# Selective scan: three PSUM banks for the decay factors, one for the row of C, written between the two sums of an index

## The chip, the cores and the metric

The kernel runs on one core of a Trainium2 chip. The metric is device time in microseconds, the median of several executions. The profile is one execution, recorded by the hardware profiler; its times start at the first instruction of the span.

## The reference

The program is a two-layer hybrid model over 16 sequences (batches b) of 512 tokens with 128 channels: attention, a recurrent feed-forward, a selective state space block, the recurrent feed-forward again, then latent attention, experts, rotary attention, experts. Only the state space block matters here, and in it only the scan:

```
def step(h, inp):
    dt_t, B_t, C_t, x_t = inp
    dA = jnp.exp(dt_t[..., None] * A[None])
    dBx = dt_t[..., None] * B_t[:, None, :] * x_t[..., None]
    h = dA * h + dBx
    y_t = jnp.sum(h * C_t[:, None, :], axis=-1)
    return (h, y_t)
...
y = jnp.moveaxis(ys, 0, 1) + Dp * xc
y = y * _silu(z)
return jnp.einsum('bti,di->btd', y, out_proj_w)
```

There are 256 inner channels and 16 state indices n. B and C have 16 rows each for a batch, one for each index, shared by all channels; A is a number for each channel and index.

## The kernel before, in words

`mamba_scan` takes the batches one after another. The 512 tokens of a batch lie along the free dimension and the 256 channels lie on 128 partitions in two halves h = 0 and 1. For each index n and half h, numbered k = 2 (16 b + n) + h, this is done:

- TensorE copies a row of B to all 128 partitions: a matmul of a selection matrix in bf16 with the three-part bf16 rows, into the one bank `b_ps` (`broadcast_b`, L1932). ScalarE copies it to SBUF (`copy_b`, L1994) into a ring of eight.
- ScalarE computes the decay factor exp(A dt) of the half into a bank of `da` in PSUM (L2032). `da` has RA = 2 banks.
- GpSimd multiplies the row of B with dt x (L2097) into `dbx`, a ring of eight.
- VectorE runs the recurrence over the tokens (`scan`, L2139) and multiplies the state with the row of C (`times_c`, L2148), which it reads straight from PSUM. TensorE has put that row there (`broadcast_c`, L1938); `c_ps` has two banks, index n uses bank n % 2.
- TensorE adds the product to the half's sum in `y_ps` with an identity matmul in fp32, which the trace shows as two passes (L1963).

Every engine runs an order written out by hand, with semaphores between the engines. The orders that matter:

- TensorE, for each n: `broadcast_b` of n + 4 (AHEAD), `broadcast_c` of n + 1, the sum of half 0, the sum of half 1; after n = 9 and n = 11 (SKIP_AT) a matmul that adds D x to one half (L1967); after n = 4 the output projection of the batch before (`outward`, L1945). `b_ps` has one bank, so a row of B waits for the copy of the one before.
- ScalarE, for each n: `copy_b` of n + 3 (COPIED), then the decay factors of (n, 0) and (n, 1). A decay factor waits until the scan that read its bank is done: `scanned` at R - RA + k + 1, where R = 8 is added at the start. From n = 4 to 10 the softplus of the next batch is strewn between.
- VectorE, for each n: the scans of both halves, then both products. At n = 0 two gates of the batch before stand between scans and products (L2155), after n = 6 the residual add (L2159), after n = 13 two step sizes of the next batch (L2130).
- GpSimd, for each n: the two products `dbx`, and the products of the next batch's set-up after n = 11 and n = 14.

`prod_ready` counts finished products (with RS = 4 added at the start), `acc_mm` finished sums, `c_mm` rows of C. The eight banks of PSUM are all taken: `da` 2, `b_ps` 1, `c_ps` 2, `y_ps` 2, `out_ps` 1. Batches 2 to 13 run in a loop of two batches a turn, the first two and the last two are written out.

Of the kernel before, what the change touches and what calls it, by code (L numbers as in the profile page):

```python
# [1843 lines left out]
def mamba_scan(core, x, mamba_dram, bc_dram, w):  # L1844
# [3 lines left out]

    R = 8
    RS = 4  # L1850
    RA = 2
    RB = 8
    AHEAD = 4
    COPIED = 3
# [2 lines left out]
    with core.phase() as ph:  # L1857
# [10 lines left out]
        state, prod = ph.sb("state", [P, RS, T]), ph.sb("prod", [P, RS, T])  # L1868
        gated = ph.sb("gated", [P, 2, T])
        da = ph.ps("da", [P, RA, T])  # L1870
        b_ps, c_ps = ph.ps("b_ps", [P, T]), ph.ps("c_ps", [P, 2, T])
        y_ps, out_ps = ph.ps("y_ps", [P, 2, T]), ph.ps("out_ps", [P, T])
        loaded = [ph.sem(f"loaded{u}") for u in range(2)]
        select_loaded = ph.sem("select_loaded")
# [20 lines left out]
        def k_slot(n, h, ring=R):  # L1895
            return (2 * n + h) % ring
# [22 lines left out]
        @block.tensor  # L1919
        def _(pe):  # L1920
            pe.sem_inc(acc_mm, RS)
            pe.sem_inc(out_mm, 1)

            def inputs_loaded(b, u):
                pe.wait_ge(loaded[u], 32 * (b // 2) + 32 if isinstance(b, int) else 16 * (b - u) + 32)

            def broadcast_b(b, u, n):

                if n == 0:
                    inputs_loaded(b, u)  # L1930
                pe.wait_ge(b_ready, STATE * b + n + 1)
                pe.matmul(b_ps[:, :], w["select"][:, n], bc[:, u], start=True, stop=True).then_inc(b_mm, 1)  # L1932

            def broadcast_c(b, u, n):
                if n == 0:
                    inputs_loaded(b, u)
                pe.wait_ge(prod_ready, RS - 4 + 2 * (STATE * b + n) + 2)
                pe.matmul(c_ps[:, n % 2], w["select"][:, STATE + n], bc[:, u], start=True, stop=True  # L1938
                          ).then_inc(c_mm, 1)

            def outward(b):
                pe.wait_ge(gated_ready, 2 + 2 * b + 2)
                pe.wait_ge(added, b + 1)
                for h in range(2):
                    mm = pe.matmul(out_ps[:, :], w["out_w"][:, h], gated[:, h], start=(h == 0), stop=(h == 1))  # L1945
                mm.then_inc(out_mm, 1)

            def sequence(b, u, first=False, last=False):
                for n in range(STATE):
                    if n + AHEAD < STATE:  # L1950
                        broadcast_b(b, u, n + AHEAD)
                    elif not last:
                        broadcast_b(b + 1, 1 - u, n + AHEAD - STATE)
                    if n + 1 < STATE:
                        broadcast_c(b, u, n + 1)
                    elif not last:
                        broadcast_c(b + 1, 1 - u, 0)
                    for h in range(2):
                        k = 2 * (STATE * b + n) + h
                        if n == 0 and not first:  # L1960
                            pe.wait_ge(gated_ready, 2 * b + h + 1)
                        pe.wait_ge(prod_ready, RS + k + 1)
                        pe.matmul(y_ps[:, h], w["ident"], prod[:, k_slot(n, h, RS)], start=(n == 0),  # L1963
                                  stop=(n == STATE - 1)).then_inc(acc_mm, 1)
                    if n in SKIP_AT:
                        h = SKIP_AT.index(n)
                        pe.matmul(y_ps[:, h], skip_w[:, h], inp[:, u, h], start=False, stop=False)  # L1967
                    if n == 4 and not first:
                        outward(b - 1)

            pe.wait_ge(select_loaded, 16)
            for n in range(AHEAD):
                broadcast_b(0, 0, n)
            broadcast_c(0, 0, 0)
            pe.wait_ge(skip_ready, 2)
            sequence(0, 0, first=True)
            sequence(1, 1)
            with pe.Fori(1, NB // 2 - 1) as i:
                for u in range(2):
                    sequence(2 * i + u, u)  # L1980
            sequence(NB - 2, 0)
            sequence(NB - 1, 1, last=True)
            outward(NB - 1)

        @block.scalar
        def _(act):
            act.preload_act_table_set("natural_log_exp_and_others")
            act.sem_inc(b_ready, 1)

            def copy_b(b, n):  # L1990
                m = STATE * b + n
                act.wait_ge(b_mm, m + 1)
                act.wait_ge(dbx_ready, 2 * m + 2)
                act.activation(b_sb[:, n % RB], b_ps[:, :], ACT.Copy).then_inc(b_ready, 1)  # L1994

            act.activation(rate[:, :, :], w["a_log"], ACT.Exp).then_inc(soft, 1)

            def magnitude(b, u, h):
                act.wait_ge(loaded[u], 32 * (b // 2) + 32 if isinstance(b, int) else 16 * (b - u) + 32)
                act.wait_ge(dt_ready, 2 * b + h + 1)  # L2000
                act.activation(small[:, h], inp[:, u, 4 + h], ACT.Abs).then_inc(soft, 1)

            def decayed(b, h):
                act.wait_ge(soft, 1 + 6 * b + 3 * h + 1)
                act.activation(small[:, h], small[:, h], ACT.Exp, scale=-1.0).then_inc(soft, 1)

            def rounded(b, h):
                act.wait_ge(soft, 1 + 6 * b + 3 * h + 2)
                act.activation(lost[:, h], small[:, h], ACT.Identity, bias=w["one"]).then_inc(back, 1)

            def returned(b, h):
                act.wait_ge(back, 4 * b + 2 * h + 1)
                act.activation(lost[:, h], lost[:, h], ACT.Identity, bias=w["one"], scale=-1.0
                               ).then_inc(back, 1)

            def logarithm(b, h):
                act.wait_ge(soft, 1 + 6 * b + 3 * h + 2)
                act.activation(log1[:, h], small[:, h], ACT.Ln, bias=w["one"]).then_inc(soft, 1)

            def sequence(b, u, last=False):  # L2020
                for n in range(STATE):
                    m = STATE * b + n
                    if n + COPIED < STATE:
                        copy_b(b, n + COPIED)
                    elif not last:
                        copy_b(b + 1, n + COPIED - STATE)
                    for h in range(2):
                        k = 2 * m + h
                        if n == 0:
                            act.wait_ge(dt_ready, 2 + 2 * b + h + 1)  # L2030
                        act.wait_ge(scanned, R - RA + k + 1)
                        act.activation(da[:, k_slot(n, h, RA)], dt[:, u, h], ACT.Exp, scale=rate[:, h, n:n + 1]  # L2032
                                       ).then_inc(da_ready, 1)
                    if last:
                        continue
                    if n == AT:
                        magnitude(b + 1, 1 - u, 0)
                    if n == AT + 1:
                        decayed(b + 1, 0)
                        rounded(b + 1, 0)  # L2040
                    if n == AT + 2:
                        returned(b + 1, 0)
                    if n == AT + 3:
                        logarithm(b + 1, 0)
                        magnitude(b + 1, 1 - u, 1)
                    if n == AT + 4:
                        decayed(b + 1, 1)
                    if n == AT + 5:
                        rounded(b + 1, 1)
                        returned(b + 1, 1)  # L2050
                    if n == AT + 6:
                        logarithm(b + 1, 1)

            act.wait_ge(rate_ready, 1)
            for h in range(2):
                magnitude(0, 0, h)
                decayed(0, h)
                rounded(0, h)
                returned(0, h)
                logarithm(0, h)  # L2060
            for n in range(COPIED):
                copy_b(0, n)
            with act.Fori(0, NB // 2 - 1) as i:
                for u in range(2):
                    sequence(2 * i + u, u)
            sequence(NB - 2, 0)
            sequence(NB - 1, 1, last=True)

# [46 lines left out]
        def _(dve):  # L2115
# [26 lines left out]
            def times_c(b, n, h):  # L2142
                k = 2 * (STATE * b + n) + h
                s = k_slot(n, h, RS)
                dve.wait_ge(scanned, R + k + 1)
                dve.wait_ge(c_mm, STATE * b + n + 1)
                dve.wait_ge(acc_mm, k + 1)
                dve.tensor_tensor(prod[:, s], state[:, s], c_ps[:, n % 2], ALU.mult).then_inc(prod_ready, 1)  # L2148

            def gate(b, u):  # L2150

# [247 lines left out]
```

## Time and profile before

| | us |
|---|---|
| median of 3 runs | 5323.51 |
| lowest and highest | 5317.22 and 5327.42 |
| profiled execution, device time | 5320.46 |
| its span, first to last instruction | 5318.7 |
| mean granted TensorE clock of the span | 0.914 of 2.4 GHz |

In the page of the profile, busy shares are of the whole span of eleven phases; the scan is one of them, about a fifth of the span. A share of the page says little about it, so the views are cut to its stretch. In these views PE is TensorE's matmuls, PEld its weight loads, DVE VectorE, ACT ScalarE, POOL GpSimd. L12 is line 12 of the kernel. The time between brackets behind a row is how long the engine had stood idle before it, and what ended that.

### The profile page before, as it was taken

The numbers are of one execution on the slowest core, as the hardware profiler recorded it, in microseconds if no ns is written. First come the engines' busy times: TensorE is split into PE (matmuls) and PEld (weight loads), VectorE is DVE, ScalarE is ACT, GpSimd is POOL, SyncE is SP. The second block draws the span as 40 slices with busy tenths as digits, with TensorE's granted clock in tenths as the row PEclk, the third lists the DMA queues.
The fourth block names the chain that finished last, engine by engine and source line by source line (L and its number), as shares of the span: only waits on it lengthen the run. The fifth ranks groups of instructions, "written<-read, shape, count | busy, mean of one in ns | idle before, by whom it ended". The sixth has DMA issues, their size and how long they took to land. (4 is left out here: it accounts for less than half of the span.)

```text
span 5318.7 us, 109649 instructions
## 1 busy us (share of the span) xinstructions
PE 4172.8 (78%) x31637; PEld 2106.4 (40%) x31638; DVE 3541.8 (67%) x8801; ACT 2850.0 (54%) x5331; POOL 1612.8 (30%) x1559
## 2 busy tenths in 40 slices
PE   6499999898667677778789999933987699983598
PEld 3144444552222222226222222323983244442497
DVE  3388888647899998984499999831116788873012
ACT  7255555676555555556667777721325466662232
POOL 3000000011777777741200000055536000006552
PEclk9699999999899998999889999966999799995799
DMA  7522222106100010000722222213665333321466
GB/s 257 150 73 72 74 76 72 33 0 216 42 26 26 26 36 28 26 13 2 244 73 74 78 76 75 72 38 123 214 189 209 108 95 96 98 77 46 142 212 191
DMA packets 546193, 502.03 MB, mean 94 GB/s; under 512 B 163774, under 2 KB 482911, under 8 KB 545788
## 3 DMA queue, kind: packets, MB, share of 16 engines
q1 hardware_dynamic: 527724, 460.95, 29.2%
q0 software_dynamic: 18160, 37.42, 2.1%
q8 instruction: 137, 2.24, 0.2%
q14 instruction: 172, 1.41, 0.1%
HBM read 330.57 MB, written 167.58 MB: 94 GB/s over the span
## 5 line engine op out<-in xcount | busy, mean ns | idle before, releaser
L1428 ACT ACTIVATE p_probs<-p_t_ps 128x512 f32<-128x512 f32 (+1 forms) x2304 | 1141.8, 551 | 680.9 <-PE p_t_ps L1320 243.8
L1963 PE MATMUL p_y_ps<-p_prod,c_ident 128*128 128x512 f32 x1024 | 554.5, 667 | 295.5 <-DVE p_prod L2148 290.9
L1333 PE MATMUL p_o_ps<-p_probs,p_v_st 128*32 128x256 f32 (+3 forms) x8704 | 727.0, 407 | 3.2 <-ACT p_o_sb L1414 2.9
L1465 DVE TENSOR_REDUCE p_row_max<-p_s_ps 128x1 f32<-128x512 f32 x1072 | 669.0, 680 | 71.9 <-PE p_s_ps L1271 55.6
L1254 POOL TENSOR_TENSOR p_v_st<-p_v_raw,p_ones 128x128 f32<-128x128 f32 x192 | 87.5, 456 | 2068.4 <-PE p_o_ps L1333 1946.9
L2097 POOL TENSOR_TENSOR p_dbx<-p_dtx,p_b_sb 128x512 f32<-128x512 f32 x512 | 632.4, 1267 | 113.2 <-ACT p_b_sb L1994 112.4
L2139 DVE TENSOR_TENSOR_SCAN p_state<-p_da,p_dbx 128x512 f32<-128x512 f32 x512 | 598.8, 1208 | 84.6 <-ACT p_da L2032 67.0
L1302 PE MATMUL p_t_ps<-p_t_q,p_t_k 50*128 50x512 bf16 (+3 forms) x3072 | 516.4, 336 | 147.6 <-ACT p_probs L1428 58.6
L1271 PE MATMUL p_s_ps<-p_s_k,p_s_q 48*128 48x512 bf16 (+3 forms) x3216 | 508.6, 340 | 146.8 <-DMA p_s_k<-stack_k 75.0
L1462 DVE CUSTOM_DVE_ANT_0 p_tried<-p_s_ps,p_s_bias 128x512 bf16<-128x512 f32 (+3 forms) x1072 | 470.5, 485 | 137.0 <-PE p_s_ps L1271 134.4
L1462 DVE CUSTOM_DVE_ANT_0 p_tried<-p_s_ps,c_mask_row 128x512 bf16<-128x512 f32 (+3 forms) x1072 | 470.5, 485 | 86.2 <-PE p_s_ps L1271 76.2
L791 DVE TENSOR_TENSOR p_y<-p_out_ps,p_raw 128x256 f32<-128x256 f32 x142 | 60.3, 425 | 581.3 <-PE p_out_ps L742 581.3
L1963 PEld LDWEIGHTS p_y_ps<-p_prod,c_ident 128*128 128x128 f32 x1024 | 188.7, 202 | 556.9 <-DVE p_prod L2148 478.3
L1994 ACT ACTIVATE p_b_sb<-p_b_ps 128x512 f32<-128x512 f32 x256 | 152.6, 596 | 430.2 <-PE p_b_ps L1932 419.4
L1302 PEld LDWEIGHTS p_t_ps<-p_t_q,p_t_k 50*128 50x128 bf16 x3072 | 149.1, 93 | 563.6 <-ACT p_probs L1428 361.5
L803 POOL DMA_INDIRECT weighed_rows<-p_y,p_raw x284 | 273.1, 962 | 296.9 <-DVE p_y L791 252.4
L2032 ACT ACTIVATE p_da<-p_dt,p_rate 128x512 f32<-128x512 f32 x512 | 337.4, 686 | 29.5 <-DVE p_state L2139 28.6
L773 ACT ACTIVATE p_hidden<-p_hid_ps 128x512 f32<-128x512 f32 x284 | 169.6, 597 | 316.0 <-PE p_hid_ps L731 313.7
L2148 DVE TENSOR_TENSOR p_prod<-p_state,p_c_ps 128x512 f32<-128x512 f32 x512 | 322.3, 670 | 0.0
L1312 PE MATMUL p_t_ps<-p_bias_parts,c_flip 64*128 64x384 bf16 (+2 forms) x4608 | 302.8, 269 | 0.0
L654 POOL DMA_INDIRECT routed_rows<-p_rows,p_index x256 | 249.2, 974 | 163.3 <-DVEq L599 86.5
L1333 PEld LDWEIGHTS p_o_ps<-p_probs,p_v_st 128*32 128x32 f32 x8704 | 174.7, 108 | 262.0 <-issue 245.4
(256 smaller groups left out, 6888.0 us busy)
## 6 DMA issues: line engine op xcount, KB each, us to landing
p_wb<-in_w SPq DMA_DIRECT2D x142, 512.0 KB
p_s_q<-stack_q SPq DMA_DIRECT2D x408, 96.0 KB
p_s_k<-stack_k SPq DMA_DIRECT2D x408, 96.0 KB
p_t_q<-stack_q SPq DMA_DIRECT2D x390, 96.0 KB
p_t_k<-stack_k SPq DMA_DIRECT2D x390, 96.0 KB
mamba_inputs<-p_out SPq DMA_DIRECT2D x17, 1536.0 KB, 5.7
p_inp<-mamba_inputs SPq DMA_DIRECT2D x17, 1536.0 KB
stack_q<-p_parts SPq DMA_DIRECT2D x51, 384.0 KB
```

Source lines behind the costliest of these rows:

```text
L1271: mm = pe.matmul(s_ps[:, banks[r], at:at + width], s_q[rows, g % 2, pair, c * P:(c + 1) * P], s_k[rows, g % 2, pair, 0:width], start=True, ...
L1302: mm = pe.matmul(out[r], t_k[rows, g % 2, pair, c * P:(c + 1) * P], t_q[rows, g % 2, pair, first:first + width], start=True, stop=not mask ...
L1312: mm = pe.matmul(out[r], bias["flip"][rows, k], bias["t"][q][rows, k, 2 * g + pair, first - c * P:first - c * P + width], start=False, sto ...
L1333: mm = pe.matmul(o_ps[32 * j:32 * j + 32, at:to], v_st[:, g % 2, c, j, :], probs[:, g % 2, j, place[c] + at - first:place[c] + to - first] ...
L1428: act.activation(exps, tile, ACT.Exp, scale=scale).then_inc(expd, 1)
L1462: read = dve.tensor_tensor_reduce(tried[:, slot, at:at + width], scores, over, 1.0, LOWEST, ALU.add, ALU.max, found)
L1465: read = dve.tensor_reduce(found, scores, X, ALU.max)
L1963: pe.matmul(y_ps[:, h], w["ident"], prod[:, k_slot(n, h, RS)], start=(n == 0), stop=(n == STATE - 1)).then_inc(acc_mm, 1)
L2032: act.activation(da[:, k_slot(n, h, RA)], dt[:, u, h], ACT.Exp, scale=rate[:, h, n:n + 1]).then_inc(da_ready, 1)
L2097: pool.tensor_tensor(dbx[:, k_slot(n, h)], dtx[:, u, h], b_sb[:, n % RB], ALU.mult).then_inc(dbx_ready, 1)
L2139: dve.tensor_tensor_scan(out=state[:, out], data0=da[:, k_slot(n, h, RA)], data1=dbx[:, s], initial=0.0, op0=ALU.mult, op1=ALU.add).then_i ...
L2148: dve.tensor_tensor(prod[:, s], state[:, s], c_ps[:, n % 2], ALU.mult).then_inc(prod_ready, 1)
```

## The change

`da` gets three banks and `c_ps` one. The row of C for n + 1 is no longer written ahead of both sums of n; its matmul stands between the sum of half 0 and the sum of half 1, behind a wait for both products of n. The decay factor waits for the scan three halves back, at n = 0 two back, since the ring of three starts anew with each batch.

```
-    RA = 2
+    RA = 3
...
-        b_ps, c_ps = ph.ps("b_ps", [P, T]), ph.ps("c_ps", [P, 2, T])
+        b_ps, c_ps = ph.ps("b_ps", [P, T]), ph.ps("c_ps", [P, T])
...
             def broadcast_c(b, u, n):
                 if n == 0:
                     inputs_loaded(b, u)
-                pe.wait_ge(prod_ready, RS - 4 + 2 * (STATE * b + n) + 2)
-                pe.matmul(c_ps[:, n % 2], w["select"][:, STATE + n], bc[:, u], start=True, stop=True
+                pe.wait_ge(prod_ready, RS + 2 * (STATE * b + n))
+                pe.matmul(c_ps[:, :], w["select"][:, STATE + n], bc[:, u], start=True, stop=True
                           ).then_inc(c_mm, 1)
...
                         broadcast_b(b + 1, 1 - u, n + AHEAD - STATE)
-                    if n + 1 < STATE:
-                        broadcast_c(b, u, n + 1)
-                    elif not last:
-                        broadcast_c(b + 1, 1 - u, 0)
                     for h in range(2):
                         k = 2 * (STATE * b + n) + h
                         if n == 0 and not first:
                             pe.wait_ge(gated_ready, 2 * b + h + 1)
                         pe.wait_ge(prod_ready, RS + k + 1)
+                        if h == 1 and n + 1 < STATE:
+                            broadcast_c(b, u, n + 1)
+                        elif h == 1 and not last:
+                            broadcast_c(b + 1, 1 - u, 0)
                         pe.matmul(y_ps[:, h], w["ident"], prod[:, k_slot(n, h, RS)], start=(n == 0),
                                   stop=(n == STATE - 1)).then_inc(acc_mm, 1)
...
-                        act.wait_ge(scanned, R - RA + k + 1)
+                        act.wait_ge(scanned, R - (RA if n else 2) + k + 1)
...
-                dve.tensor_tensor(prod[:, s], state[:, s], c_ps[:, n % 2], ALU.mult).then_inc(prod_ready, 1)
+                dve.tensor_tensor(prod[:, s], state[:, s], c_ps[:, :], ALU.mult).then_inc(prod_ready, 1)
```

## Rows read from the trace of the kernel before

**Rows 1.** Engines over stretches: stretch, length, busy us (instructions), clock, DMA.

```profile
1734.30:1737.90 3.60, 3.57 (x4) 1.33 (x5) 3.60 (x5) 0.00 (x0) 3.60 (x3) 0.50 0.69 215
...
1339.00:2369.00 1030.00, 727.08 (x1664) 266.61 (x1664) 936.12 (x1104) 560.25 (x925) 756.69 (x608) 0.93 0.08 26
```

**Rows 2.** Grouped instructions of the scan: busy, mean ns, idle before and releasers.

```profile
L2139 DVE TENSOR_TENSOR_SCAN p_state<-p_da,p_dbx 128x512 f32<-128x512 f32 x512 | 598.8, 1208 | 84.6 <-ACT p_da L2032 67.0 <-issue 9.0 <-POOL p_dbx L2097 8.5
...
L2148 DVE TENSOR_TENSOR p_prod<-p_state,p_c_ps 128x512 f32<-128x512 f32 x512 | 322.3, 670 | 0.0
...
L1963 PEld LDWEIGHTS p_y_ps<-p_prod,c_ident 128*128 128x128 f32 x1024 | 188.7, 202 | 556.9 <-DVE p_prod L2148 478.3 <-issue 65.7 <-DVE p_gated L2155 9.9
...
L1938 PEld LDWEIGHTS p_c_ps<-p_bc,xn 96*128 96x128 bf16 x254 | 26.7, 105 | 96.2 <-issue 85.0 <-DVE p_prod L2148 11.2
```

**Rows 3.** Who waited for whom in the scan: us in total, times, longest.

```profile
ACT p_b_sb L1994 <- PE p_b_ps L1932: 417.2, 228, 5.4
...
DVE p_state L2139 <- ACT p_da L2032: 67.0, 70, 1.7
...
ACT p_da L2032 <- DVE p_state L2139: 28.6, 54, 3.1
```

**Rows 4.** An ordinary step in order of time: start, length, engine, line.

```profile
1745.71 1.26 DVE L2148 TENSOR_TENSOR p_prod<-p_state,p_c_ps 128x512 f32<-128x512 f32 x2
...
1746.42 1.98 PE L1963 MATMUL p_y_ps<-p_prod,c_ident 128*128 128x512 f32 x4 [1.01 <-DVE p_prod L2148]
...
1748.24 0.38 PE L1932 MATMUL p_b_ps<-p_bc,xn 96*128 96x512 bf16 x1
...
1748.46 0.38 PE L1938 MATMUL p_c_ps<-p_bc,xn 96*128 96x512 bf16 x1
...
1748.74 0.60 ACT L1994 ACTIVATE p_b_sb<-p_b_ps 128x512 f32<-128x512 f32 x1 [1.09 <-PE p_b_ps L1932]
...
1749.24 1.30 ACT L2032 ACTIVATE p_da<-p_dt,p_rate 128x512 f32<-128x512 f32 x2
...
1749.85 1.98 PE L1963 MATMUL p_y_ps<-p_prod,c_ident 128*128 128x512 f32 x4 [1.01 <-DVE p_prod L2148]
...
1750.31 2.33 DVE L2139 TENSOR_TENSOR_SCAN p_state<-p_da,p_dbx 128x512 f32<-128x512 f32 x2
```

**Rows 5.** The step with the output projection, in order of time.

```profile
1751.67 1.88 PE L1945 MATMUL p_out_ps<-p_gated,c_out_w 128*128 128x512 f32 x4
...
1753.39 0.38 PE L1932 MATMUL p_b_ps<-p_bc,xn 96*128 96x512 bf16 x1
...
1754.38 1.29 ACT L2032 ACTIVATE p_da<-p_dt,p_rate 128x512 f32<-128x512 f32 x2
...
1755.25 2.34 DVE L2139 TENSOR_TENSOR_SCAN p_state<-p_da,p_dbx 128x512 f32<-128x512 f32 x2 [1.44 <-ACT p_da L2032]
```

**Rows 6.** A step with a skip product, in order of time.

```profile
1705.95 1.02 PE L1967 MATMUL p_y_ps<-p_inp,p_skip_w 128*128 128x512 f32 x2
...
1708.68 2.34 DVE L2139 TENSOR_TENSOR_SCAN p_state<-p_da,p_dbx 128x512 f32<-128x512 f32 x2 [0.58 <-ACT p_da L2032]
```

**Rows 7.** Behind a batch boundary, in order of time.

```profile
1734.33 3.78 PE L1963 MATMUL p_y_ps<-p_prod,c_ident 128*128 128x512 f32 x4 [4.31 <-DVE p_prod L2148]
...
1737.90 0.63 PE L1932 MATMUL p_b_ps<-p_bc,xn 96*128 96x512 bf16 x1
...
1738.33 0.63 PE L1938 MATMUL p_c_ps<-p_bc,xn 96*128 96x512 bf16 x1
...
1738.66 0.60 ACT L1994 ACTIVATE p_b_sb<-p_b_ps 128x512 f32<-128x512 f32 x1 [5.43 <-PE p_b_ps L1932]
...
1740.03 2.34 DVE L2139 TENSOR_TENSOR_SCAN p_state<-p_da,p_dbx 128x512 f32<-128x512 f32 x2 [1.73 <-ACT p_da L2032]
```

**Rows 8.** The skip step of another batch: decay pair and scan.

```profile
1907.79 1.29 ACT L2032 ACTIVATE p_da<-p_dt,p_rate 128x512 f32<-128x512 f32 x2
...
1909.02 2.34 DVE L2139 TENSOR_TENSOR_SCAN p_state<-p_da,p_dbx 128x512 f32<-128x512 f32 x2 [0.93 <-ACT p_da L2032]
```

## The prediction

> **What bounds the kernel now.** I read the views from the outside in. The table of engines over stretches of the span comes first. The diff touches the scan phase alone, so I cut to it, 1339 to 2369 us, where VectorE is busy 936 of 1030 us and TensorE 727 [rows 1]. VectorE is the engine to follow. The grouped list of VectorE's instructions says how much it stands still: 84.6 us before its scans and nothing at all before its products with C [rows 2]. The list of waits says for whom: 67.0 us in 70 waits for ScalarE's decay factor (L2032) [rows 3]. ScalarE in turn waited 417.2 us for the row of B out of TensorE (L1932), but only 28.6 us for a scan to free a bank of `da` [rows 3]. So before costing anything: the ring of `da`, which the change lengthens, is the short wait, and the row of B, whose place in TensorE's queue the change alters, is the long one.
>
> The timeline shows how the two hang together. An ordinary step of an index n takes 3.43 us (sums begin at 1746.42 and again at 1749.85) [rows 4]. In it TensorE starts the two sums 0.71 us after the products begin (1746.42), starts the row of B 1.82 us later (1748.24), ScalarE copies that row 0.50 us after (1748.74), and starts the decay pair 0.50 us after that (1749.24) [rows 4]. ScalarE is in order, so `copy_b(n+3)` stands ahead of the exponential that the scan of n needs. How soon may the scan follow? Where it did wait, it began 0.87 us after the decay pair began (1754.38 to 1755.25) [rows 5]. From products to the scan two indices on, that chain is 0.71 + 1.82 + 0.50 + 0.50 + 0.87 = 4.40 us; VectorE's own work between the same two points is 1745.71 to 1750.31, 4.60 us [rows 4]. The ordinary step therefore hides the chain with 0.20 us to spare, and no more.
>
> It doesn't hide where TensorE has something extra before the row of B. With the output projection (n = 4) B starts at 1753.39, after 1.72 us more, and the scan stalls 1.44 us [rows 5]; there are 15 such, of 1.20 to 1.44 us. With a skip product (n = 9 and 11) B starts two passes of 0.43 us later and the scan stalls 0.58 us [rows 6]; 31 such, of 0.34 to 0.93 us. Just after a batch boundary TensorE has stood idle 4.31 us, its granted clock in the next 3.6 us is 0.50, that is 1.2 GHz, B follows the start of the sums after 3.57 us instead of 1.82, and the scan stalls 1.73 us [rows 1, 7]; 14 stalls of this kind at index 2 and about 10 at other places. These are the 70 waits.
>
> **The change part by part.** *Moving C's row.* TensorE's order was B(n+4), C(n+1), sum 0, sum 1; it becomes B(n+4), sum 0, C(n+1), sum 1. No instruction is added or taken away: 256 rows of C, 256 of B, 1024 passes of the sums as before. But C used to run while TensorE was going to wait for a product anyway: after C at 1748.46 its next work came at 1749.85 [rows 4]. Now it runs between the sums, in front of sum 1 and all that is queued behind it: skip product, output projection, and B(n+5). Its price is the distance from B to C at full clock, 1748.24 to 1748.46, 0.22 us [rows 4]; at half clock 1737.90 to 1738.33, 0.43 us [rows 7]. Is there a gap between the sums that it could fill? The projection, which is four passes as the two sums are, takes 1.72 us to the start of B, four times 0.43 [rows 5], and the sums take the same after a start of 0.10; so there is none. Its own weight load should hide: C may go once the second product is done, which is 1.26 us after the products begin, while sum 0 ends at about 0.71 + 0.10 + 0.86 = 1.67 us [rows 4].
>
> What each place pays, by kind of stall: 15 projections at 0.22 = 3.3 us. Skips: of 31, six have a stall of 0.93 us whose scan starts 1.23 us after its decay pair (1907.79 to 1909.02) where 0.87 would do [rows 8], so something of VectorE's own, 0.36 us long, covers the delay there; the other 25 at 0.22 = 5.5 us. The 24 stalls at half clock: between 0.22 and 0.43 each, since the clock often rises within the same pair; I take 0.33 = 8 us, ends 5.3 and 10.3. One gate that waits for sum 1 of the batch before: 0.4 us. An ordinary step loses its 0.20 us of slack to a 0.22 us delay; a stall of 0.02 us then gives the next step cover, so at most one in two of some 80 steps without other cover pays: under 1 us. Sum 3.3 + 5.5 + 8 + 0.4 + 0.8 = 18 us. What remains just hidden is worth naming: VectorE's extra instructions (gates, step sizes, the residual add) cover indices 0, 1, 7, 8, 14 and 15.
>
> *One bank for C.* C(n+1) can no longer be written before both products of n are read. It must be there when VectorE wants it, 3.43 us after the products of n began. At full clock it is: it starts at about 1.67 us and a consumer follows 0.50 us after a start (B at 1748.24, copy at 1748.74) [rows 4], so 2.2 us, with 1.2 us to spare. At half clock sum 0 takes 1.71 + 0.15 us, C starts at 0.71 + 1.86 = 2.57 us and its reader may follow 0.76 us later (1737.90 to 1738.66) [rows 7]: 3.33 us, 0.1 us to spare. Cost nothing; if this cover goes, it is the rival below. Perfetto Trace Analysis of the Trainium skill, section Matmuls, speaks against this edit: independent matmul groups should rotate through different PSUM banks, so that one is read out while the next is written. By that rule the reader of each of 256 rows of C would wait out the 0.50 us from its start to its use, 128 us in all; by the arithmetic on the rows above it waits for none. No run here shows it yet.
>
> *Three banks for the decay factors.* The exponential of (n, 0) now waits for the scan three halves back, not two. That removes up to 28.6 us of ScalarE's waiting [rows 3]. None of it, as far as I can see, is on the path. In the ordinary step the decay pair starts 1.00 us after the row of B and runs on; in the step of the projection, whose scan stalls, 0.99 us after it [rows 4, 5]: had a scan held it there, it would have come later. The copy is held by TensorE, and a third bank doesn't bring the row of B any sooner. Ends: 0 and 28.6 us saved; I take 0, by these two rows. At n = 0 the code keeps a distance of two.
>
> The profiled execution took 5320.5 us, 1.8 beyond its span and 3.1 below the median of 5323.5. 5320.5 + 18 = 5338.5 on its own footing, 5341 against the median.
>
> **Rivals.**
> (a) *The third bank pays.* If ScalarE, freed from waiting for scans, kept a lead over VectorE, the stalls would shrink. For it: 54 such waits, 28.6 us. Against: ScalarE's lead ends at each copy, which waited 228 times for TensorE [rows 3]. Its price is at most 28.6 us, so 5323.5 - 28.6 = 5295 us if C's delay also hid; it outweighs the delay once more than 18 of the 28.6 us lie on the path. This one ends faster.
> (b) *The delay vanishes.* If C's row in fact finds a hole between the sums, because the second product comes late, the time stays at 5323.5. For it: the second product is done only 0.4 us before sum 0 ends, by the 1.26 and 1.67 us above. Against: that is still before.
> (c) *C's weight load isn't hidden*, or the single bank makes C miss its reader. Each step would pay C's load and the reload for sum 1 on top, 0.105 + 0.202 us, about 0.3 [rows 2]. 64 stalled steps x 0.3 = 19 us, and the ordinary steps, their slack gone, some three per batch x 16 x 0.3 = 14 us: 5341 + 33 = 5374 us. Against: the load may start at 1.26 us and is wanted at 1.67.
>
> **How the numbers follow.** Forecast, the row of B comes later by C's time: 0.68, centre 5341. (a) 0.08, (b) 0.14, (c) 0.10; of the last, 0.02 is for a wait of 0.50 us on every row of C, 256 x 0.50 = 128 us on top. Within the forecast the half-clock stretches, which account for about 27 us of stalls before, may fall otherwise: 8 us either way, which with the bounds gives 5327 to 5352. The range 5321 to 5364 takes in the forecast, (b) and the lower part of (c). A measurement of this kernel can tell about 0.2%, 10.6 us, from no change. Faster by that: (a), 0.08. Slower: 0.93 of the forecast and (c), 0.63 + 0.10 = 0.73. Same: 0.19.
>
> **What would show it.** In the profile after, on TensorE the order sum 0, C, sum 1, with B's row 2.04 us after the sums begin instead of 1.82 in an ordinary step. VectorE's stall after the projection grows from 1.44 to about 1.66 us, after a skip from 0.58 to 0.80 us; its idle time before scans goes from 84.6 to about 102 us, and the idle time before the products with C stays near nothing. ScalarE's wait for a scan falls from 28.6 us to less than half while VectorE's time doesn't follow. The forecast is wrong if the stalls keep their sizes, if the products begin to wait for C (rival c), or if scans that waited for the decay factor no longer do (rival a).

## The result and the profile after

| | before, us | after, us |
|---|---|---|
| median | 5322.15 (5 runs) | 5374.41 (5 runs) |
| lowest and highest | 5317.08 and 5327.42 | 5369.56 and 5378.81 |
| span of the profiled execution | 5318.7 | 5372.6 |
| mean granted TensorE clock of the span | 0.914 | 0.906 |

The ratio is 1.0100, with an interval of 1.0086 to 1.0114: 52 us slower. The forecast was slower, 5341 us, in a range of 5321 to 5364. The sign is right; the loss was put at a third of what it is, and the measured time lies outside the range.

The groups of VectorE's instructions in the scan after the change (columns as in [rows 2]), then the waits (as in [rows 3]), then the stretch of 1030 us (as in [rows 1]):

```profile
L2139 DVE TENSOR_TENSOR_SCAN p_state<-p_da,p_dbx 128x512 f32<-128x512 f32 x512 | 598.9, 1208 | 132.7 <-ACT p_da L2032 118.5 <-POOL p_dbx L2097 9.7 <-issue 4.4
L2148 DVE TENSOR_TENSOR p_prod<-p_state,p_c_ps 128x512 f32<-128x512 f32 x512 | 322.1, 669 | 0.0
```

```profile
DVE p_state L2139 <- ACT p_da L2032: 118.5, 83, 2.8
...
ACT p_da L2032 <- DVE p_state L2139: 7.9, 8, 2.5
```

```profile
1339.00:2369.00 1030.00, 725.10 (x1582) 266.52 (x1583) 894.21 (x1053) 534.16 (x893) 735.97 (x592) 0.89 0.08 26
```

VectorE's idle time before scans went from 84.6 to 132.7 us [rows 2], by 48.1 of the 53.9 us that the span grew. The scan phase, from the start of its first scan to the end of its last product, grew by 49.2 us, from 1012.9 to 1062.1; the other 4.7 us lie outside it, in work that the change doesn't touch, and are no more than runs of one kernel differ by. VectorE's work itself is the same to 0.2 us. Nothing waits for C: the products' idle time is 0.0, with one bank as with two. ScalarE's waits for a scan fell from 28.6 us in 54 to 7.9 us in 8 [rows 3], so the third bank did its part, and VectorE's time didn't follow. The clock's mean over the stretch fell from 0.93 to 0.89 [rows 1].

An ordinary step after the change, on TensorE:

```profile
1782.99 1.12 PE L1963 MATMUL p_y_ps<-p_prod,c_ident 128*128 128x512 f32 x2 [2.12 <-DVE p_prod L2148]
...
1783.96 0.38 PE L1938 MATMUL p_c_ps<-p_bc,xn 96*128 96x512 bf16 x1
...
1784.18 1.02 PE L1963 MATMUL p_y_ps<-p_prod,c_ident 128*128 128x512 f32 x2
...
1785.04 0.38 PE L1932 MATMUL p_b_ps<-p_bc,xn 96*128 96x512 bf16 x1
```

Sum 0, C, sum 1, B. C starts 0.97 us after the first sum, as the two passes end, and the second sum 0.22 us later; B comes 2.05 us after the sums begin, where it was 1.82 [rows 4]. The stalls that answer to [rows 5] and [rows 6]:

```profile
1771.46 2.34 DVE L2139 TENSOR_TENSOR_SCAN p_state<-p_da,p_dbx 128x512 f32<-128x512 f32 x2 [1.66 <-ACT p_da L2032]
...
1791.18 2.34 DVE L2139 TENSOR_TENSOR_SCAN p_state<-p_da,p_dbx 128x512 f32<-128x512 f32 x2 [0.77 <-ACT p_da L2032]
```

1.44 became 1.66 and 0.58 became 0.77 us: the delay of C's 0.22 us arrives at VectorE, as forecast. It isn't the whole story. I added up VectorE's stalls before scans from the timeline by the index at which they stand, over all 16 batches:

| index n | before, us | after, us | difference |
|---|---|---|---|
| 0 (batch boundary, turns of the loop) | 16.9 | 25.0 | 8.1 |
| 2 | 17.9 | 24.0 | 6.1 |
| 6 (projection) | 20.9 | 24.3 | 3.4 |
| 8 and 9 | 7.0 | 12.5 | 5.5 |
| 11 (skip) | 8.5 | 11.7 | 3.2 |
| 13 (skip) | 10.3 | 32.2 | 21.9 |
| 15 | 3.0 | 3.1 | 0.1 |

Index 6 and 11 carry what the forecast gave them. Index 8, which the forecast counted among the places that VectorE's extra instructions cover, stalls in 13 batches. Index 13 carries 21.9 us, which the forecast didn't foresee: in 11 of the 16 batches its stall is 2.49 to 2.85 us. This is one, in order of time:

```profile
1725.65 1.12 PE L1963 MATMUL p_y_ps<-p_prod,c_ident 128*128 128x512 f32 x2 [1.86 <-DVE p_prod L2148]
...
1726.62 0.56 PE L1938 MATMUL p_c_ps<-p_bc,xn 96*128 96x512 bf16 x1
...
1726.97 1.91 PE L1963 MATMUL p_y_ps<-p_prod,c_ident 128*128 128x512 f32 x2
...
1728.68 1.73 PE L1967 MATMUL p_y_ps<-p_inp,p_skip_w 128*128 128x512 f32 x2
...
1730.24 0.38 PE L1932 MATMUL p_b_ps<-p_bc,xn 96*128 96x512 bf16 x1
...
1732.11 2.34 DVE L2139 TENSOR_TENSOR_SCAN p_state<-p_da,p_dbx 128x512 f32<-128x512 f32 x2 [2.50 <-ACT p_da L2032]
```

```profile
1725.80:1730.20 4.40, 4.40 (x7) 1.66 (x8) 3.82 (x5) 0.00 (x0) 2.36 (x2) 0.61 0.00 0
```

The second sum takes 1.71 us to the start of the skip product, twice its 0.86, the skip product 1.56: B comes 4.59 us after the first sum, and the scan stalls 2.50 us. The granted clock over those 4.40 us is 0.61, so most of them pass at the lower level, 1.2 GHz. Added up from the record of the granted clock, the scan spent 126 us at half clock before and 201 us after. Both leave out its first 7 to 8 us, which are at half clock in every run.

### The profile page after: what moved, and what is told of

Same layout as the page of the kernel before. It is cut to its first block and busy times, and to the rows that moved or that the text cites. A ratio compares the mean times of both kernels' runs of the same rounds, so it can differ in the third digit from the quotient of the medians.

```text
span 5372.6 us, 109718 instructions
## 1 busy us (share of the span) xinstructions
PE 4217.9 (79%) x31637; PEld 2123.6 (40%) x31638; DVE 3542.0 (66%) x8801; ACT 2843.3 (53%) x5331; POOL 1616.0 (30%) x1559
## 5 line engine op out<-in xcount | busy, mean ns | idle before, releaser
L1963 PE MATMUL p_y_ps<-p_prod,c_ident 128*128 128x512 f32 x1024 | 621.6, 692 | 311.9 <-DVE p_prod L2148 310.5
L2139 DVE TENSOR_TENSOR_SCAN p_state<-p_da,p_dbx 128x512 f32<-128x512 f32 x512 | 598.9, 1208 | 132.7 <-ACT p_da L2032 118.5
L1271 PE MATMUL p_s_ps<-p_s_k,p_s_q 48*128 48x512 bf16 (+3 forms) x3216 | 509.1, 340 | 145.0 <-DMA p_s_k<-stack_k 74.1
```

The lines of the kernel that those rows point to most:

```text
L1271: mm = pe.matmul(s_ps[:, banks[r], at:at + width], s_q[rows, g % 2, pair, c * P:(c + 1) * P], s_k[rows, g % 2, pair, 0:width], start=True, ...
L2139: dve.tensor_tensor_scan(out=state[:, out], data0=da[:, k_slot(n, h, RA)], data1=dbx[:, s], initial=0.0, op0=ALU.mult, op1=ALU.add).then_i ...
```

## The experiments

Three parts of the change could carry the loss: the order of TensorE (theory O), the ring of decay factors (R), the single bank of C (S). Within O, the loss beyond the 18 us of the forecast could be the clock's (K). And if so, the clock could react to the slower pace (P) or to C's place among the sums (Q). The runs were made in four sets, each with its own runs of the kernel before beside it, whose medians were 5273.2, 5273.7, 5320.7 and 5321.3 us. So ratios are compared, not times. The sets differ outside the scan phase: the rest of the profiled execution takes 4258 to 4266 us in the first two sets and 4306 to 4315 us in the other two and the first measurement. So the length of the scan phase alone can be compared across sets. "Half clock" is the time of the scan at half clock, added up as above; "idle" is VectorE's before scans; "phase" is the length of the scan phase. The last three come from one profiled execution of each run. "Order alone" below is the changed kernel with `RA = 2`.

| run | ratio | interval | idle, us | half clock, us | phase, us |
|---|---|---|---|---|---|
| before, first measurement | 1 | | 84.6 | 126 | 1012.9 |
| the change, first measurement | 1.0100 | 1.0086 to 1.0114 | 132.7 | 201 | 1062.1 |
| e8, the change again | 1.0089 | 1.0072 to 1.0106 | 135.8 | 205 | 1065.9 |
| e1, order alone | 1.0094 | 1.0077 to 1.0111 | 133.1 | 198 | 1063.0 |
| e6, place alone, two banks of C | 1.0099 | 1.0082 to 1.0116 | 133.1 | 201 | 1062.7 |
| e2, before, copy behind | 0.9867 | 0.985 to 0.9883 | 16.9 | 72 | 938.7 |
| e3, after, copy behind | 0.9866 | 0.985 to 0.9883 | 17.0 | 68 | 939.1 |
| e4, before, filled | 0.9979 | 0.9969 to 0.9988 | 74.1 | 61 | 1001.4 |
| e5, order alone, filled | 1.0016 | 1.0007 to 1.0026 | 91.3 | 92 | 1018.9 |
| e7, two rows of C between | 1.0105 | 1.0088 to 1.0122 | 135.0 | 167 | 1067.0 |
| e9, small copy on ScalarE | 1.0046 | 1.0029 to 1.0063 | 109.5 | 184 | 1038.3 |
| e10, two small copies | 1.009 | 1.0073 to 1.0107 | 129.1 | 205 | 1059.1 |
| e11, copy behind and filled | 0.9862 | 0.9846 to 0.9879 | 16.9 | 58 | 938.7 |

**Which part: the ring?** The ring of decay factors put back to two:

```
-    RA = 3
+    RA = 2
```

> The change with the ring of decay factors put back to two banks: C in one bank, written between the two sums, is all that is left. Theory O (the order of TensorE, with what its clock makes of it): the ring of three does nothing, so 5374 us within 5, VectorE idle before scans about 130 us, as with the whole change. Theory R (the third bank of decay factors does harm, for instance by moving ScalarE's work): a good part of the loss goes, 5322 to 5350 us. If the third bank helped and hid part of the loss: above 5385 us.

> The changed kernel as it stands, once more, on the chip that ran the order alone. If the third bank of decay factors does nothing, its ratio to before is that of the order alone, 1.009, within 0.002. If the third bank gives something back or takes it: 0.3% or more away.

The order alone costs 1.0094, the whole change 1.0089 and 1.0100. The two ran on different chips, not on one as the second expectation has it, so each is compared with the kernel before beside it; their scan phases, 1063.0 us for the order alone and 1062.1 and 1065.9 us for the change, say the same. ScalarE's waits for a scan are back at 36.9 us in 88 in the order alone, against 7.9 us; VectorE's idle time is the same within 3 us. The third bank removes waits that nobody is waiting behind. R falls.

**Which part: the single bank?** The kernel before with nothing but the place of C changed; two banks of C stay:

```
-                    if n + 1 < STATE:
-                        broadcast_c(b, u, n + 1)
-                    elif not last:
-                        broadcast_c(b + 1, 1 - u, 0)
...
                         pe.wait_ge(prod_ready, RS + k + 1)
+                        if h == 1 and n + 1 < STATE:
+                            broadcast_c(b, u, n + 1)
+                        elif h == 1 and not last:
+                            broadcast_c(b + 1, 1 - u, 0)
```

> The kernel before with C's matmul between the two sums and nothing else changed: C keeps its two banks, the ring its two. Theory O (place alone): the whole loss, ratio 1.009, idle time before scans about 130 us. Theory S (the single bank takes part): clearly less, 1.003 to 1.006.

```profile
L2139 DVE TENSOR_TENSOR_SCAN p_state<-p_da,p_dbx 128x512 f32<-128x512 f32 x512 | 598.9, 1208 | 133.1 <-ACT p_da L2032 118.9 <-POOL p_dbx L2097 9.8 <-issue 4.4
```

The place alone has the whole loss, 1.0099, and VectorE's idle time is that of the change. The products waited for nothing there either. The single bank costs nothing that these runs can see.

**Is B's row the path?** ScalarE's copy of B's row moved behind the two decay factors, in the kernel before (e2) and in the changed one (e3):

```
-                    if n + COPIED < STATE:
-                        copy_b(b, n + COPIED)
-                    elif not last:
-                        copy_b(b + 1, n + COPIED - STATE)
                     for h in range(2):
...
                                        ).then_inc(da_ready, 1)
+                    if n + COPIED < STATE:
+                        copy_b(b, n + COPIED)
+                    elif not last:
+                        copy_b(b + 1, n + COPIED - STATE)
```

> The kernel before, with one edit: ScalarE's copy of B's row n + 3 stands behind the two decay factors of n, not ahead of them. Theory O says that all of VectorE's 67 us of waits for the decay factor come through this copy, which waits for B's row: they should nearly vanish (under 10 us), half clock or not, and the time falls by about 60 us to 5262 (5250 to 5275). The stalls at the turn of the loop, 17 us at index 0, stay. If the waits have another source (the ring of two, the scan itself), the time stays near 5322 us.

> The changed kernel with the same edit: the copy behind the two decay factors. Theory O: with the copy off the path C's new place costs nothing, so the time is that of the kernel before with the same edit, within 10 us (about 5262). Theory S (the single bank makes C miss its reader where the clock is at half): products wait for C in half-clock stretches and it is 15 to 40 us slower than that one, 5277 to 5300 us, with the idle time in front of VectorE's products, not of its scans.

VectorE's group in e2, then its two groups in e3:

```profile
L2139 DVE TENSOR_TENSOR_SCAN p_state<-p_da,p_dbx 128x512 f32<-128x512 f32 x512 | 599.9, 1213 | 16.9 <-POOL p_dbx L2097 12.5 <-issue 4.4
```

```profile
L2139 DVE TENSOR_TENSOR_SCAN p_state<-p_da,p_dbx 128x512 f32<-128x512 f32 x512 | 599.8, 1213 | 17.0 <-POOL p_dbx L2097 12.6 <-issue 4.4
L2148 DVE TENSOR_TENSOR p_prod<-p_state,p_c_ps 128x512 f32<-128x512 f32 x512 | 324.1, 677 | 0.3 <-PE p_c_ps L1938 0.3
```

The releaser "ACT p_da" is gone from the list, with its 67.0 us. Every wait of VectorE for a decay factor came through the copy in front of it. Both kernels are 70 us faster than before, and they are the same: with the copy off the path, C's place, its single bank and the third bank together cost 0.3 us of waiting (the medians, 5202.96 and 5203.59, can't be told apart). The single bank's price shows here and is that 0.3 us, one wait at a half-clock stretch, so S falls too.

**The clock.** Two more rows of 0.22 us per index where TensorE is idle anyway. In the kernel before (e4) C's row is written three times in its old place; in the order alone (e5) two rows go into the free bank behind B's:

```
+                for _ in range(2):
+                    pe.matmul(c_ps[:, n % 2], w["select"][:, STATE + n], bc[:, u], start=True, stop=True)
                 pe.matmul(c_ps[:, n % 2], w["select"][:, STATE + n], bc[:, u], start=True, stop=True
                           ).then_inc(c_mm, 1)
```

```
                 pe.matmul(b_ps[:, :], w["select"][:, n], bc[:, u], start=True, stop=True).then_inc(b_mm, 1)
+                for _ in range(2):
+                    pe.matmul(fill_ps[:, :], w["select"][:, n], bc[:, u], start=True, stop=True)
```

> The kernel before, with each row of C written three times in a row into the same bank instead of once: 2 x 0.22 us more work for TensorE per index, put where it is idle for 1.0 us, ahead of the sums and behind B's row. Nothing that VectorE waits for moves at full clock. Theory K (a large part of the loss is half-clock stretches that come from TensorE's idle time): the half-clock time of the scan falls from 126 us, the clock's mean in the scan rises from 0.93, and the time falls to 5300 to 5315 us. If the clock doesn't react to it: 5322 us within 5; if the filling gets in the way: above 5330 us.

> The order of the change (one bank of C, written between the sums, two banks of decay factors), and behind each row of B two more rows of 0.22 us into the bank that is free, where TensorE is otherwise idle for about a microsecond. It is the filling of the filled kernel of before, so the two differ by C's place alone. Theory K (the direct cost of C's place is the predicted 18 us, the rest of the loss is more time at half clock): the stalls at index 6 and 11 stay at 1.66 and 0.77 us, the large ones at index 13 and those at 8 shrink towards 0.8 and 0, half-clock time falls from about 200 us to under 100, and the time is 15 to 25 us above the filled kernel of before, a ratio to before of 1.001 to 1.003. If the loss is not the clock's, the kernel stays at a ratio of 1.009.

The stretch of 1030 us in e4, then the stall at index 13 of batch 2 in e5:

```profile
1339.00:2369.00 1030.00, 813.44 (x2204) 314.09 (x2205) 938.37 (x1109) 570.80 (x940) 756.55 (x607) 0.96 0.08 26
```

```profile
1525.10 2.34 DVE L2141 TENSOR_TENSOR_SCAN p_state<-p_da,p_dbx 128x512 f32<-128x512 f32 x2 [1.15 <-ACT p_da L2034]
```

Work that nobody needs makes the kernel before 12.5 us faster by the medians, through the clock: TensorE is busy 813 us of the stretch instead of 727, and the clock's mean is 0.96 instead of 0.93 [rows 1]. In the order alone it takes 0.8% off, 1.0094 to 1.0016; the stalls of 2.5 to 2.85 us at index 13 are gone and those at index 8 too. What is left between the two filled kernels is 5281.3 - 5260.7 = 20.6 us (two sets, whose medians of the kernel before are 0.5 us apart), 17.2 us of idle time and 17.5 us of the scan phase by the profiles. That is C's place with less help of the clock, 31 us more at half clock instead of 75, and it is near the forecast's 18 us. K holds. One more thing stands in the last row: that stall was 0.93 us before, where the forecast let 0.36 us of cover hide the delay. It is 1.15, 0.22 more. The cover didn't hide the delay.

**More of the same delay.** C's row twice between the sums:

```
+                pe.matmul(c_ps[:, :], w["select"][:, STATE + n], bc[:, u], start=True, stop=True)
                 pe.matmul(c_ps[:, :], w["select"][:, STATE + n], bc[:, u], start=True, stop=True
                           ).then_inc(c_mm, 1)
```

> The order of the change with C's row written twice between the sums, so B's row comes another 0.22 us later. Directly: 64 stalled places x 0.22 = 14 us, and now the ordinary steps have no slack left, some three per batch x 16 x 0.22 = 10 us: 24 us over the order alone, a ratio to before of 1.014. If half-clock time grows with the stalls, as theory K has it, another 10 to 30 us: 1.016 to 1.020. If the loss is not in B's delay: 1.009.

```profile
1496.13 2.34 DVE L2140 TENSOR_TENSOR_SCAN p_state<-p_da,p_dbx 128x512 f32<-128x512 f32 x2 [0.16 <-DVE p_prod L2149]
...
1504.94 2.34 DVE L2140 TENSOR_TENSOR_SCAN p_state<-p_da,p_dbx 128x512 f32<-128x512 f32 x2 [1.88 <-ACT p_da L2033]
```

```profile
1339.00:2369.00 1030.00, 755.72 (x1817) 284.31 (x1817) 890.06 (x1046) 540.34 (x892) 732.06 (x588) 0.91 0.08 26
```

The direct part came, if smaller than expected: the stall after the projection is 1.88 us, 0.22 more, and 21 scans of ordinary steps that never waited now wait 0.16 us, 3.3 us in all. The total did not: 1.0105 where 1.014 and more was expected by every theory that puts the loss in B's delay. The interval even takes in the 1.009 that was named for a loss that isn't there; the longer stalls, and e2 and e3, speak against that. Half-clock time fell from 198 to 167 us and gave the direct part back. But this run changes two things at once. The second row of C delays B, and it is also 0.22 us more work for TensorE per index: TensorE is busy 756 us of the stretch, 723 in the order alone. In e4 and e5 such work alone lowered half-clock time. So the fall to 167 us may be the filling's, and e7 doesn't say what more delay by itself does.

**The same delay elsewhere.** The kernel before with TensorE's order untouched, and one small copy of 32 columns on ScalarE (e9), or two (e10), between its wait for B's row and the copy:

```
                 act.wait_ge(dbx_ready, 2 * m + 2)
+                act.activation(junk[:, n % RB], rate[:, :, :], ACT.Copy)
+                act.activation(junk2[:, n % RB], rate[:, :, :], ACT.Copy)
```

> The kernel before, TensorE's order untouched; ScalarE does a small copy of 32 columns between its wait for B's row and the copy of that row, some 0.2 us. The delay is then the same as the change's, but on ScalarE. Theory P (the pace: longer stalls of VectorE leave TensorE idle longer, and its clock goes down more often): stalls grow by about 0.2 us each, half-clock time grows from 126 towards 200 us, large stalls appear at index 8 and 13, ratio 1.007 to 1.010. Theory Q (the place of C among the sums is what the clock reacts to): the direct part alone, 18 to 25 us, half-clock time as before, ratio 1.003 to 1.005.

> The kernel before with two of the small copies on ScalarE between its wait for B's row and the copy. One of them delayed the decay factor by 0.11 us and made the kernel 0.46% slower; two should delay it by 0.22 us or a little more, the change's own delay, with TensorE's order still untouched. Theory P (the pace): the ratio of the change, 1.009 within 0.002, half-clock time about 200 us, the stall after the projection 1.66 to 1.75 us. Theory Q (the place among the sums adds its own): no more than 1.006.

The stall at index 13 of batch 2 in e9, then the stalls after the projection and at index 13 in e10:

```profile
1526.78 2.34 DVE L2141 TENSOR_TENSOR_SCAN p_state<-p_da,p_dbx 128x512 f32<-128x512 f32 x2 [2.74 <-ACT p_da L2034]
```

```profile
1500.84 2.34 DVE L2142 TENSOR_TENSOR_SCAN p_state<-p_da,p_dbx 128x512 f32<-128x512 f32 x2 [1.67 <-ACT p_da L2035]
...
1531.17 2.34 DVE L2142 TENSOR_TENSOR_SCAN p_state<-p_da,p_dbx 128x512 f32<-128x512 f32 x2 [2.86 <-ACT p_da L2035]
```

The single copy delayed the decay factor by 0.11 us (the stall after the projection is 1.55 us), half of what I had meant. By its time e9 falls where Q had put it, 1.0046 and 25 us, and outside P's 1.007 to 1.010. But Q's number is met by chance, since it supposed twice the delay and half-clock time as before: the 25 us that it costs are far more than 70 stalls x 0.11 = 8 us, half-clock time is 184 us, and the large stall at index 13 is there. With the change's own delay, e10 has the change's ratio, its idle time, its half-clock time and its stalls, without a single instruction of TensorE moved. P holds and Q falls: the clock reacts to the delay wherever it stands, not to C's place. With TensorE's own work as it was, half-clock time goes from 126 us without a delay to 184 at 0.11 us and 198 to 205 at 0.22 us. These times are of one profile each, but the mean granted clocks of all runs go the same way: 0.911 to 0.916 in the runs of the kernel before beside them, 0.907 to 0.910 in e9, 0.906 to 0.909 in e10.

**Both edits that helped.**

> The kernel before with both edits that helped: ScalarE's copy behind the decay pair, and two more rows of C in TensorE's idle time. With the copy off the path the clock has nothing left to cost (VectorE's idle time before scans was 17 us, the turns of the loop), so the filling brings nothing more: the ratio of the copy edit alone, 0.987, within 0.002. If half-clock stretches still cost something there: 0.984 or less.

0.9862 against 0.9867: the same, as are the scan phases, 938.7 us both. With the copy behind the pair the clock has nothing left to cost that these runs can see. The version to keep is e2, the kernel before with four lines moved, 1.3% faster than before and 2.3% faster than the changed kernel.

## Why the prediction was right or wrong

- *The bound and the path* (VectorE, held by the decay factor, held by the copy, held by B's row): right. e2 removes the copy from it, and 67.0 us of waits vanish.
- *C's price at full clock, 0.22 us, with its weight load hidden*: right. B comes 2.05 us after the sums where 2.04 was said, the stalls are 1.66 and 0.77 us where 1.66 and 0.80 were said.
- *The ordinary step just keeps hiding the chain*: right for the change; with a second 0.22 us it no longer does (e7).
- *VectorE's extra instructions cover indices 0, 1, 7, 8, 14 and 15*: wrong at 8 and 0. Where TensorE is at half clock the cover is too short: index 8 stalls 0.68 to 1.04 us in 13 batches, and the waits for the decay factor at index 0 grew from 2.4 to 13.6 us.
- *The six skip stalls of 0.93 us have cover*: wrong by 6 x 0.22 = 1.3 us. In the filled pair they went from 0.93 to 1.15. The 0.36 us seem to be added behind the decay factor, not beside it; why, these traces don't show.
- *The 24 stalls at half clock grow by 0.22 to 0.43 us each, 8 us in all, and otherwise "may fall otherwise: 8 us either way"*: this is the step that failed. I took the number of half-clock stretches as given and let it vary evenly around that, as if the delay itself did not act on the clock. It does: half-clock time grew from 126 to 201 us here, and to 205 us where the same delay was put on ScalarE (e10). Of the 48.1 us at the scans, index 6 and 11 and some 3.4 us of index 13 are 10 us of the direct part; the filled pair, whose half-clock time differs by only 31 us, puts the whole of the forecast's mechanism at 17 to 21 us, with the half-clock stalls at 0 and 2 as the rest of it. The other 30 us are new half-clock stretches and their stalls: 18.5 us of them at index 13, the rest at 0, 2 and 8. (The forecast's own lower end, 5327, doesn't follow from its bounds either: 5341 - 8 - 2.7 is 5330; nothing hangs on it.)
- *The third bank pays nothing*: right (e1 against e8 and the first measurement). Rival (a) falls.
- *C reaches its reader from one bank*: right, e6 against e1, and 0.3 us in e3. The rule of the Trainium skill (Perfetto Trace Analysis, section Matmuls) that matmul groups should rotate through different PSUM banks would have given 128 us; no run here agrees. At full clock the row has 1.2 us to spare; at half clock the forecast left it 0.1 us, and there the products do begin to wait, 0.3 us in e3 and, with two rows, 1.1 us in e7, of which the profile puts 0.3 us to C.
- *Rival (b)*, the delay vanishes: falls. *Rival (c)* has the measured time as its number, 5374 us, and is wrong all the same: C's weight load is hidden (C 0.97 us after the first sum, the second sum 0.22 us after that) and no product waits. A number met by chance proves no mechanism.

What stays open: what exactly makes the clock fall. A delay of 0.11 us brings 184 us at half clock, 0.22 brings 198 to 205, 0.44 together with 0.22 us more work of TensorE brings 167, and filling 0.43 us per index without a delay brings 61. That the delay raises half-clock time is shown by e10 and e9; that it does so by leaving TensorE idle for longer is an inference from these runs and not shown, and why the stretches settle at certain indices isn't known. The Trainium skill (TensorE: Matmul & The Clock Gate, section "A second HAM failure mode: psum-queue depth-cycling") tells of a kernel in which short idle times between groups of matmuls made the clock swing between its two levels; the trace agrees as far as that goes, with 201 us at half clock in 52 stretches against 126 us in 28.

## What to carry to other kernels

When a wait on the critical path grows and TensorE idles in that wait, price the stretches at half clock again and let the range reach further upward than downward; they grew by 75 us here and nearly tripled a loss of some 18 us. An experiment that lengthens a delay by more work on TensorE changes the clock by that work too (e7); put the delay on another engine, as e10 does. Follow a stall back through each in-order queue to the first instruction that is needed later than the one behind it: here it was ScalarE's copy, needed three indices later, in front of a decay factor needed at once, and moving it was worth 70 us where more banks were worth nothing. A ring that removes waits of an engine that isn't late saves nothing.

## What the runs showed of the hardware that was not expected

- Useless matmuls made the kernel faster: 0.43 us per index of extra rows in TensorE's idle time took half-clock time in the scan from 126 to 61 us and 12.5 us off the median (0.9979, interval 0.9969 to 0.9988), and 0.8% off the order alone.
- After the change the half-clock stretches fall at the same indices in nearly every batch (from index 6 in 13 batches, from 12 in 11, and near the boundary), where before four batches had one from index 6 and none from 12; the stalls of one batch then repeat to 0.01 us in the next but one, 1.63, 1.66, 1.04, 0.77 and 2.50 us.
- A copy of 32 columns on ScalarE, 0.23 us long in its row, put in front of another copy delayed what followed by only 0.11 us (stall 1.44 to 1.55 us).
